# Eight matmuls of the identity, laid-out ids and a split table load at the start of a DLRM tower

## The reference

```python
e = jnp.stack([tbl_0[ids[:, 0]], tbl_1[ids[:, 1]], ..., tbl_25[ids[:, 25]]], axis=1)
combined = jnp.concatenate([e, r_dense_x[:, None, :]], axis=1)       # 2048 x 27 x 128
interact = jnp.einsum('bfd,bgd->bfg', combined, combined)
z = interact[:, _TRIU_I, _TRIU_J]                                    # 2048 x 351
h = jnp.concatenate([z, r_dense_x], axis=1)
h = jnp.maximum(h @ W_top1 + b_top1, 0.0)                            # 479 -> 512
h = jnp.maximum(h @ W_top2 + b_top2, 0.0)                            # 512 -> 256
y = h @ W_top3                                                       # 256 -> 1
```

## Time and profile before

| | |
|---|---|
| median of three runs | 369.92 us (368.41 to 370.58) |
| span of the profiled execution | 368.7 us |
| TensorE matmuls busy | 339.9 us (92%) |
| TensorE weight loads busy | 282.4 us (77%) |
| GpSimd busy | 259.5 us (70%) |
| ScalarE busy | 187.5 us (51%) |
| VectorE busy | 170.0 us (46%) |
| gathers issued by GpSimd | 256, mean 1009 ns |

### The profile page before, as it was taken

The page is one execution under the profiler, slowest core; times in us unless marked ns, Lnnn a source line. Parts: engine busy times, 40 slices in busy tenths (PEclk is TensorE's granted clock), DMA queues, the critical chain, the costliest instruction groups (busy, mean ns, idle before and its releaser), DMA issues.

```text
span 368.7 us, 12553 instructions
## 1 busy us (share of the span) xinstructions
PE 339.9 (92%) x5616; PEld 282.4 (77%) x5616; DVE 170.0 (46%) x388; ACT 187.5 (51%) x260; POOL 259.5 (70%) x265
## 2 busy tenths in 40 slices
PE   1999889698999999999999999999999999889677
PEld 0488877586888888887888788888888888877576
DVE  3599955555254635356255535356255534202020
ACT  2399831553636734583627634483627633564313
POOL 6788877777777777777777777777777777776000
PEclk9999999999999999999999999999999999999989
DMA  6969394244243333423242334424232222222000
GB/s 231 338 198 245 95 281 129 54 114 94 58 118 80 81 94 100 103 71 112 66 110 80 89 87 100 106 70 110 65 111 80 66 52 73 54 53 72 3 4 1
DMA packets 19369, 37.33 MB, mean 101 GB/s; under 512 B 5525, under 2 KB 8213, under 8 KB 19316
## 3 DMA queue, kind: packets, MB, share of 16 engines
q1 hardware_dynamic: 11124, 19.74, 18.6%
q0 software_dynamic: 8192, 16.79, 17.4%
HBM read 36.51 MB, written 0.01 MB: 99 GB/s over the span
## 4 chain that ended last, share of the span: by engine, by line
POOL 57%; issue 20%; PE 13%; DVE 5%; DMA 3%; ACT 2%; POOLq 0%; SPq 0%
POOL rows L263 57%; DVE onehot L298 3%; PE ps_lk L552 3%; PE ps_lk L576 2%; PE ps_gram L602 2%; DMA h<-in_tbl 2%; PE ps_lk L657 2%; DVE table L304 1%; DMA rows<-in_tbl,gather_ids 1%; PE ps_lk L672 1%; PE ps_mlp L636 1%; PE ps_zt L629 1%; ACT xt L374 0%; PE ps_zt L636 0%; PE ps_mlp L629 0%
## 5 line engine op out<-in xcount | busy, mean ns | idle before, releaser
L263 POOL DMA_INDIRECT rows<-in_tbl,gather_ids x256 | 258.2, 1009 | 79.7 <-issue 77.1
L298 DVE TENSOR_SCALAR onehot<-ids 128x512 fp32r<-128x512 f32 (+1 forms) x328 | 126.8, 442 | 84.0 <-PE ps_lk L576 51.2
L576 PE MATMUL ps_lk<-onehot,table 128*128 128x512 f32 (+1 forms) x704 | 155.3, 374 | 4.5 <-DVE onehot L298 3.4
L576 PEld LDWEIGHTS ps_lk<-onehot,table 128*128 128x128 f32 x704 | 120.5, 190 | 25.7 <-issue 5.3
L384 ACT COPY xt<-ps_tr 128x512 f32<-128x512 f32 x64 | 76.8, 1200 | 73.9 <-PE ps_tr L587 73.9
L312 DVE STREAM_TRANSPOSE zs<-ps_gram 128x832 f32<-128x832 f32 x16 | 16.8, 1050 | 99.9 <-PE ps_gram L602 99.9
L602 PEld LDWEIGHTS ps_gram<-xt 128*26 128x26 f32 x4096 | 44.0, 104 | 23.3 <-issue 20.3
L602 PE MATMUL ps_gram<-xt 128*26 128x26 f32 x4096 | 53.0, 193 | 9.2 <-issue 4.8
L371 ACT COPY xt<-ps_lk 128x512 f32<-128x512 f32 x35 | 42.0, 1235 | 21.6 <-issue 9.6
L587 PE MATMUL ps_tr<-ident,rows 128*128 128x128 f32 x256 | 39.4, 276 | 2.6 <-DMA rows<-in_tbl,gather_ids 2.3
L587 PEld LDWEIGHTS ps_tr<-ident,rows 128*128 128x128 f32 x256 | 29.9, 140 | 9.5 <-issue 4.0
(11 more groups left out here) (59 smaller groups left out, 157.6 us busy)
## 6 DMA issues: line engine op xcount, KB each, us to landing
ids<-in_ids_onehot SPq DMA_DIRECT2D x41, 256.0 KB
rows<-in_tbl,gather_ids POOLq DMA_INDIRECT x256
w<-in_tbl SPq DMA_DIRECT2D x6, 512.0 KB, 6.7
zt<-in_tbl SPq DMA_DIRECT2D x3, 512.0 KB, 7.0
dense_x<-in_dense SPq DMA_DIRECT2D x8, 128.0 KB
zt<-in_dense SPq DMA_DIRECT2D x8, 128.0 KB, 2.7
h<-in_tbl SPq DMA_DIRECT2D x1, 512.0 KB, 6.1
w<-in_w SPq DMA_DIRECT2D x1, 512.0 KB
```

Source lines behind the costliest of these rows:

```text
L263: pool.indirect_dma_start(rows[n % ROW_BUFS][:, r, :], None, t_[f"tbl_{GATHERED[r]}"], bass.IndirectOffsetOnAxis(ap=gather_ids[:, n, r:r + ...
L298: nc.vector.tensor_scalar(onehot[:, k, 0:w], ids[e % IDS][:, 0:w].bitcast(F32), float(k), None, ALU.is_equal).then_inc(s_unit, 1)
L576: m = nc.tensor.matmul(ps_lk[e % LB][:, x], table[:, i, part, k, :], onehot[:, k, x], start=(k == 0 and j == 0 and part == 0), stop=(k == ...
```

## The change

Three edits. The ids of the first step, which were one row of 512 read by a broadcast, now lie in HBM 128 times, a copy for each partition, and are loaded as an ordinary 128 x 512 array. The load of the first table becomes two transfers: the blocks k = 0 and 1 (LEADERS) with the old semaphore, the other six with a semaphore of their own, for which the first lookup waits at k = 2, and the conversion of that table on ScalarE as well. And TensorE, once the identity is there, multiplies it by itself eight times into a bank that isn't in use yet.

```diff
+LEADERS = 2
+WARM = 8
...
+        s_raw_rest = sem("s_raw_rest")
...
             def load_ids(e):
...
+                if e == 0:
+
+                    sp.dma_start(ids[0][:, :], t_["ids_first"]).then_inc(s_ids[0], 16)
+                    return
...
             def load_raw(j):
...
-                sp.dma_start(raw[j][:, :, :], t_[f"tbl_{ONE_HOT[j]}"].rearrange("(p k) d -> p k d", k=KT)
-                             ).then_inc(s_raw[j], 16)
+                rows_of = t_[f"tbl_{ONE_HOT[j]}"].rearrange("(p k) d -> p k d", k=KT)
+                if j == 0:
+                    sp.dma_start(raw[0][:, 0:LEADERS, :], rows_of[:, 0:LEADERS, :]).then_inc(s_raw[0], 16)
+                    sp.dma_start(raw[0][:, LEADERS:KT, :], rows_of[:, LEADERS:KT, :]).then_inc(s_raw_rest, 16)
+                    return
+                sp.dma_start(raw[j][:, :, :], rows_of).then_inc(s_raw[j], 16)
...
             def high(n):
                 j = SPLIT[n]
                 act.wait_ge(s_raw[j], 16)
+                if j == 0:
+                    act.wait_ge(s_raw_rest, 16)
...
             def lookup_first():
...
                     pe.wait_ge(s_unit, k + 1)
+                    if k == LEADERS:
+                        pe.wait_ge(s_raw_rest, 16)
...
             pe.wait_ge(s_ident, 2)
+            for i in range(WARM):
+
+                nc.tensor.matmul(ps_mlp[:, 0:P], ident[:, :], ident[:, :], start=True, stop=True)
             lookup_first()
...
+    arrays["ids_first"] = np.ascontiguousarray(np.broadcast_to(arrays["ids_onehot"][0], (P, N)))
```

## The result

The change took 367.01 us (median of 11 runs, 365.58 to 368.24) where the kernel before took 370.13 (11 runs, 367.44 to 372.14): ratio 0.9928, 95% interval 0.9902 to 0.9953. That is 3.1 us faster by the medians and 2.7 by the ratio, where 3.3 (a median of 366.7) had been forecast. The profiled execution of the change took 365.58 us with a span of 363.8, so some 1.8 us lie around a span.

The account below looks back on a forecast made before the run. GpSimd's gather 248, then TensorE's tail, were taken to set the end. From the span of 368.7 us, 0.82 (GpSimd) and 2.45 (tail hole) came off, giving 365.4, or a median of 366.7; range 364.9 to 369.9.

Parts of the forecast that it names:

- What bounds the kernel: Whole kernel: GpSimd's gather 248, then TensorE's 36 us tail, set the end; TensorE without GpSimd would win 0.40 us at most.
- The hole in the tail: First Gram product of TensorE's tail: 33 added instructions move a packet border, so the 2.23 us idle goes; 2.45 us won.
- GpSimd: -0.82 forecast: Ninth gather: it no longer waits for the first lookup and starts at 14.07 instead of 14.89; 0.82 us won.
- gathers stretched beside VectorE: GpSimd's gathers hit by VectorE's subtractions: two fewer or more are 1.9 us either way; value taken 0.
- The start: Start of program: ids at 3.75 us (other bound 6.55), identity matmuls until 5.5, first lookup from 5.6 instead of 7.92.
- From the span to the median: Conversion of the profiled span, 368.7 us, to the runs' median, 369.92: the 1.2 us difference is carried.
- The first (the hole stays): Tail: the fetch still hangs on the Gram product's wait, or borders move otherwise; only GpSimd's wait goes, 369.1 us; chance 0.22.
- The second (nothing at the start): Start: ids no faster and gathers hit twice more; 369.1 us, or 371.5 with the hole kept; chance 0.08.
- The third (worse borders): Steady part: moved borders make Gram products wait 2.23 us each; slower, 373.4 us with five; chance 0.05.
- The fourth (half clock in the tail): Last tile: TensorE idles up to 2.5 us, then a low clock costs 1.9 us; 368.6 us; chance 0.10.

Follow-up runs that it names:

- e3: The change without its eight matmuls of the identity, one instruction more than the kernel before; 369.81 us, ratio 0.9993.
- e6: The change with 63 small 26x26 matmuls instead of the eight, 253 instructions more than the kernel before; 369.13 us, ratio 0.9963.
- e8: The change itself run and profiled again, beside other kernels on one chip; 367.09 us, ratio 0.9934.
- e2: The change plus 56 small matmuls early in the program, 257 instructions more than the kernel before in all; 371.46 us, ratio 1.0030.
- e5: The kernel before with LEAD[1] = 1: the ninth gather waits for two k of the first lookup instead of four; 369.90 us, ratio 0.9989.
- e9: The kernel before with three 26x26 matmuls (12 instructions) ahead of early transposes; 369.70 us, ratio 0.9986.
- e1: The kernel before with 32 useless TensorE instructions (eight 26x26 matmuls) ahead of early transposes; 367.24 us, ratio 0.9927.
- e4: The kernel before with the eight matmuls of the identity alone, old ids and table transfer; 367.85 us, ratio 0.9952.
- e10: The change with the first step's ids read by the broadcast as before; 367.62 us, ratio 0.9951.
- e11: The change with the first table in one transfer of 512 KB; 367.70 us, ratio 0.9939.
- e12: The change without its eight matmuls of the identity, a second execution with a profile; it took 365.52 us.
- e7: The change with the eight matmuls of last1(0, 3) moved ahead of the last Gram product; 366.77 us, ratio 0.9903.

## Why the prediction was right, point by point

**What bounds the kernel.** GpSimd up to gather 248 and TensorE's tail behind it: so it is again in the profile of the change, where TensorE waits 0.52 us for that gather's rows at 330.39, although its first lookup ended five us sooner. What it won at the start went into such waits (4.0 us in all, 2.3 before). But of the fourteen profiles only four have a wait there (before 0.40, the change 0.52, e3 0.48, e6 0.82). In the other ten the rows are there when TensorE comes, and TensorE sets the end. The second profile of the change (e8, span 364.3 us) is one of them:

```profile
326.13 0.95 POOL L274 DMA_INDIRECT rows<-in_tbl,gather_ids  x1 [0.30 <-issue]
...
330.65 0.60 PE L602 MATMUL ps_tr<-ident,rows 128*128 128x128 f32 x4
```

In such an execution an earlier gather 248 is worth nothing at the end. The prediction took the limit of one execution for that of the kernel. The tail stands behind either limit, so its term does not depend on this.

**The hole in the tail: -2.45 forecast, -3.0 measured in the profiled pair.** From the start of the first Gram product to the end of the second it was 7.46 us before (355.59 - 348.13) and is 4.46 (350.74 - 346.28). Over the profiles with the old order of the tail it is 7.46 to 7.83 with the hole (before, e2, e5, e6, e9) and 4.46 to 4.70 without (the change, e1, e3, e4, e8, e10, e11, e12). That TensorE reaches a border before its packet is shown: useless instructions alone give the gain (e1), the change without the moved border loses much of it (e6), and the hole, or its successor in the second product, stands where the count of 256 puts it (after 123 matmuls of the first product for no instruction added, 124 for 253, 117 for 12, 122 for 257; after 99 of the second for 32, 98 for 33, 114 for 1). The size was off by 0.55: 3.4 us had been allowed from request to use, so that TensorE would go on 4.57 us after the first product's start (352.7 - 348.13), and it went on after 4.05 (350.33 - 346.28). That the 98 matmuls ahead of the new stop took 1.0 us instead of 1.3 only made the stop longer. Over many executions the border is worth 2.0 us (e6 against e8) to 3.1 (e1 against before) by the medians, 1.1 to 2.7 by the ratios.

**GpSimd: -0.82 forecast, -1.23 at gather 248 in the profiled pair, small and unsure on average.** The wait went, and the ninth gather started 0.08 us from the forecast. The value of 0 for gathers stretched beside VectorE held: four of the first 32, as before. But 0.82 was the wait of one execution; in e1, with the old start, it was absent. Gather 248 starts at 327.73 in one profile of the change and at 326.13 in the other, so the 1.23 us are within what differs between executions of one kernel. And an earlier gather counts only where TensorE waits for it at the end. e5, which takes only this wait away, can't be told from zero (-0.6 to 1.4 us by its interval), nor can e3, which has the early ids and the split without the eight matmuls; e6, which has the start without the border, is 0.3 to 2.5 us under before; and e1 gets as much as the change with nothing of the start. It should have stood as a bound, with the value somewhere between it and nothing.

That the sum came so close (3.3 us forecast, 3.1 by the medians) is in part luck: the tail's term was 0.55 too small in the profiled pair, and GpSimd's 0.82 is not established in the average.

**The start.** Ids at 4.42 us (3.75 forecast, 6.55 the other bound; 3.86 to 4.42 in the kernels with the new ids), the eight matmuls until 5.4 (5.5), the lookup from 5.89 (5.6). The clock had doubled by 6.40 (a weight load in 0.19 us), which had been left open; the lookup ended at 13.0, and what that alone is worth at the end no run tells.

**From the span to the median.** I took the span of 368.7 for the execution's time and carried 1.2 us to the median. With the 1.8 us that lie around a span the execution had taken some 370.5, above the median of 369.92. The carrying came out right because it moved a difference and not a time. The pair of spans shows -4.9 us: 1.84 ahead of the transposes for gather 248 (332.23 - 330.39) and 3.0 behind them. Of the 4.9, 1.4 are that the change's profiled execution was the fastest of its eleven (365.58 against 367.01).

**The rivals.** The first (the hole stays) is not what the change does, but what it says of the request is real: with twelve instructions instead of 33 the packet still comes only behind the product's wait (e9). So the term rested on how far the border moved, and the prediction had no row for how far is enough. The second (nothing at the start) is wrong about the ids themselves, which came 1.2 to 2.8 us sooner, but with the old ids the time can't be told from the change's (e10). The third (worse borders) has its stops: the change itself has one of 2.12 us, where the kernel before waited 1.89 us for rows (at 56.03),

```profile
54.64 0.25 PE L617 MATMUL ps_gram<-xt 128*26 128x26 f32 x6 [2.12 <-issue]
```

and e1, e2, e4, e7, e8, e10 and e11 have one of 2.16 to 3.03 us there. In the profile of the change TensorE still waits for rows later on (0.52 us at 330.39), so its lead pays for the stop there; in e8 no wait for rows follows, and what the stop costs there is not shown. The change won in spite of it. The fourth (half clock in the tail) didn't show in the change: between the two Gram products the granted clock is 1.00 (columns as in the earlier trace rows, which had 0.56):

```profile
347.45:348.55 1.10, 1.10 (x18) 0.97 (x8) 0.00 (x0) 0.00 (x0) 0.00 (x0) 1.00 0.05 15
```

In e4 it is 0.50 from 353.4 to 356.8, behind the stop of 1.00 us in the second product; so a tail without the hole isn't always free of it.

## What to carry to other kernels

A gap with nothing to wait for, at a fixed count of instructions from others of its kind, with a packet of the instruction queue inside it, is a place in the program and not in the data. (The releaser "issue" alone is not enough: the 1.30 us ahead of the Gram product have it too.) Any edit ahead of the gap moves it, and here 32 instructions that do nothing made the kernel some 3 us faster. So before an edit is credited, try as many neutral instructions in its stead (e1), and the edit with the border put back (e6). Where the gap falls on the path that sets the end, longer work ahead of it can fill it (e7), though here that gain over the change is not shown. And a limit read from one execution, such as a wait of 0.40 us near the end, needs a second profile of the same kernel before a term is built on it.

## What the runs showed of the hardware

From the start of the packet to the next instruction of TensorE it is 2.25 to 2.44 us in eleven stops of the tail (before 349.12 to 351.56, change 348.00 to 350.33) and 2.60 to 2.72 in four (e9, both of e5, the second of e2). "Instruction fetch mechanics" on the page "Runtime: NRT & Kernel Launch" of the Trainium skill calls the crossing of a block mostly hidden. The trace of the change agrees for most of its 44 packets; three have a stop of more than 0.25 us (0.38, 2.12 and 0.75). The 256 instructions of a Gram product take 1.26 us, less than the 2.3 us from packet to use.

When the packet is asked for is not settled. Counted by the shift, a border 42 or 43 instructions ahead of the first Gram product brought it 3.6 to 3.9 us ahead of that product in every profile (e1, e4, e7, e8, e10, e11, the change). At about 7, 10 and 22 it came 0.86 to 1.05 us after the product's start (e6; before and e5; e9). At 11 it came 1.32 after it in one kernel (e2) and 2.5 and 2.8 ahead of it in two executions of another (e3, e12). So the place of the border alone doesn't explain it.

The 256 KB of the first step's ids reached ScalarE at 5.62 to 6.64 us where one row was read 128 times, and at 3.86 to 4.42 where they lay in HBM once for every partition.

A gather that began 0.06 to 0.14 us behind one of VectorE's subtractions of 1.21 us took 1.89 to 1.97 us instead of 0.94 (four in the kernel before, four in the change).
